# Last attention tiles and the next stages of a vision-transformer block: roots in three batches, a scale worked out early, a matrix inversion moved among products

## The reference

```python
h = patches @ w + b, with the class rows and the positions             # 32 x 38 x 256
h = h + attention(layernorm(h))                                        # 16 heads of 16, causal, q and k normalised
xn = layernorm(h) * gamma + beta
abel_out = gelu(xn @ abel_w + abel_b)
logits = xn @ moe_gate_w + moe_gate_b
topw, topi = top_k(logits, 2); topw = softmax(topw)                    # 8 experts
moe_out = sum over the two experts e of topw * (gelu(xn @ ew1[e] + eb1[e]) @ ew2[e] + eb2[e])
for i in range(3):
    moe_out = moe_out @ expm(gens[i])                                  # 256 x 256 generators
gate = sigmoid(concat(abel_out, moe_out) @ gc_w + gc_b)
out = h + abel_out * (1 - gate) + moe_out * gate
```

## Time and profile before

| | us |
|---|---|
| median of 3 runs | 394.57 (394.08 to 399.01) |
| the profiled execution | 394.72 |
| its span, from first to last instruction | 392.7 |
| TensorE busy in the span | 345.1 (88%) |
| VectorE, ScalarE, GpSimd busy | 214.8, 178.5, 151.4 |

### The profile page before, as it was taken

The page is one execution under the profiler, slowest core; times in us unless marked ns, Lnnn a source line. Parts: engine busy times, 40 slices in busy tenths (PEclk is TensorE's granted clock), DMA queues, the critical chain, the costliest instruction groups (busy, mean ns, idle before and its releaser), DMA issues.

```text
span 392.7 us, 6931 instructions
## 1 busy us (share of the span) xinstructions
PE 345.1 (88%) x2080; PEld 293.1 (75%) x2080; DVE 214.8 (55%) x581; ACT 178.5 (45%) x423; POOL 151.4 (39%) x168
## 2 busy tenths in 40 slices
PE   2998999769899999679986999999999999794894
PEld 2786454469788888556865899989999999693793
DVE  0237368797999999868785458421221123100175
ACT  1000354588998897335224844334434434341231
POOL 1002804050754663711041447653547446642000
PEclk9999899968999999969989999999999999989599
DMA  8741411133111100274222645523443444531442
GB/s 268 269 140 44 188 58 55 54 97 114 46 48 47 46 33 2 93 335 156 84 69 80 181 121 154 163 93 88 149 149 106 149 151 156 151 103 47 144 144 86
DMA packets 20544, 45.76 MB, mean 117 GB/s; under 512 B 2150, under 2 KB 12836, under 8 KB 20260
## 3 DMA queue, kind: packets, MB, share of 16 engines
q1 hardware_dynamic: 17732, 37.78, 29.1%
q0 software_dynamic: 2496, 6.82, 5.2%
q10 hardware_dynamic: 288, 0.81, 0.7%
HBM read 38.18 MB, written 7.22 MB: 116 GB/s over the span
## 4 chain that ended last, share of the span: by engine, by line
PE 75%; DVE 10%; issue 7%; DMA 3%; ACT 2%; POOL 1%; DVEq 0%; ACTq 0%; POOLq 0%; SPq 0%
PE banks L1422 11%; PE banks L1362 11%; PE banks L1431 10%; PE banks L1205 5%; PE banks L1175 5%; PE banks L1282 5%; PE banks L1258 4%; PE banks L1491 3%; PE banks L1300 3%; PE banks L1333 3%; PE banks L1501 2%; PE banks L1245 2%; PE banks L1191 2%; PE banks L1210 2%; PE banks L1231 2%
## 5 line engine op out<-in xcount | busy, mean ns | idle before, releaser
L1422 PE MATMUL banks<-qn_sb,w_sb 128*128 128x128 f32 x416 | 51.6, 278 | 1.0 <-ACT qn_sb L624 1.0
L624 ACT ACTIVATE qn_sb<-banks,col_sb 128x128 f32<-128x128 f32 x52 | 21.1, 458 | 66.1 <-PE banks L1409 66.1
L1431 PE MATMUL banks<-w_sb,sq_sb 128*128 x208 | 50.0, 385 | 0.3 <-ACT sq_sb L635 0.3
L1422 PEld LDWEIGHTS banks<-qn_sb,w_sb 128*128 128x128 f32 x416 | 49.2, 194 | 1.3 <-ACT qn_sb L624 1.2
L452 POOL DMA_INDIRECT y_rows<-pT_sb,sidx_sb x26 | 26.0, 999 | 56.7 <-DVE pT_sb L1097 55.5
L1431 PEld LDWEIGHTS banks<-w_sb,sq_sb 128*128 128x128 f32 x208 | 39.7, 194 | 5.7 <-issue 0.5
L1097 DVE TENSOR_TENSOR pT_sb<-banks,p_sb 128x256 f32<-128x256 f32 x26 | 11.0, 425 | 51.0 <-PE banks L1431 48.3
L635 ACT ACTIVATE sq_sb<-banks,col_sb 128x128 f32<-128x128 f32 x104 | 32.6, 369 | 12.9 <-PE banks L1422 10.8
L1175 PE MATMUL banks<-wtok_sb,patch_sb 128*114 128x256 f32 x132 | 30.4, 393 | 7.1 <-DMA wtok_sb<-in_w_tok 7.0
L446 POOL DMA_INDIRECT qn_sb<-z_rows,gidx_sb x26 | 27.4, 1054 | 21.1 <-PE banks L1409 14.1
L1175 PEld LDWEIGHTS banks<-wtok_sb,patch_sb 128*114 128x114 f32 x132 | 24.3, 186 | 12.8 <-DMA patch_sb<-in_patches 6.9
(11 more groups left out here) (204 smaller groups left out, 668.8 us busy)
## 6 DMA issues: line engine op xcount, KB each, us to landing
w_sb<-in_w SPq DMA_DIRECT2D x26, 512.0 KB
w_sb<-in_w SPq DMA_DIRECT2D x1, 4096.0 KB, 12.6
patch_sb<-in_patches SPq DMA_DIRECT2D x11, 342.0 KB, 3.0
vrep_sb<-v_rows SPq DMA_DIRECT2D x33, 114.0 KB
qk_sb<-y_rows SPq DMA_DIRECT2D x10, 228.0 KB
v_rows<-v_sb SPq DMA_DIRECT2D x11, 114.0 KB
z_rows<-h_sb SPq DMA_DIRECT2D x11, 114.0 KB
out_rows<-h_sb SPq DMA_DIRECT2D x10, 114.0 KB
```

The lines of the kernel that those rows point to most:

```text
L624: last = nc.scalar.activation(xsT_sb[:, (2 * s + c) * 128:(2 * s + c + 1) * 128], bank[1][:, c * 128:(c + 1) * 128], ACT.Identity, scale=c ...
L1422: last = nc.tensor.matmul(bank[2 + 2 * s + c // 2][:, (c % 2) * 128:(c % 2 + 1) * 128], w1_sb[:, w0:w0 + 128], xsT_sb[:, (2 * s + k) * 128 ...
L1431: last = nc.tensor.matmul(bank[6 + s][:, 0:D], hidT_sb[:, s * HID + k * 128:s * HID + (k + 1) * 128], w2_sb[:, ds(e * 4 * D + k * D, D)], ...
```

## The change

The roots (`powers`) are taken in three batches, tiles 0 to 6, 7 to 9 and 10 (`CUT = (7, 10)`), and the first comes ahead of `gather_images(9)` on GpSimd. The generators' scale is worked out by VectorE just ahead of the attention loop, and ScalarE multiplies by it, one copy at the end of each of its steps 8 and 9. VectorE prepares the first batch of roots after tile 8, puts `norm_z(0)` and `norm_z(1)` ahead of `select(10)`, and has the rest of the z stage in another order. On TensorE and ScalarE `turn_att(10)`, `output(10)` and `keep_attT(10)` stand later in the z stage; `rank()` comes after product 0 and `invert()` after product 6.

```diff
+        CUT = (7, 10)
 # GpSimd
             for t in range(NT):
+                if t == NT - 1:
+                    powers(1, 0, CUT[0])
                 if t >= 1:
                     gather_images(t - 1)
...
-            powers(1, 0, 8)
             gather_images(NT - 1)
-            powers(2, 8, NT)
+            powers(2, CUT[0], CUT[1])
+            powers(3, CUT[1], NT)
 # ScalarE, end of attn_step
+                if isinstance(t, int) and t in (8, 9):
+                    scale_generators(t - 8)
+
+            def scale_generators(n):
+                act.wait_ge(d_gen, 32)
+                act.wait_ge(scale_set, 1)
+                m = (a_sb, aT_sb[:, :])[n]
+                nc.scalar.activation(m, m, ACT.Copy, scale=nrm_sb[:, 12:13]).then_inc(n_scaled, 1)
 # ScalarE, z stage
             for t in range(NT):
-                if t == 3:
+                if t == 4:
                     keep_attT(NT - 1)
                 keep_zT(t, t % 2)
 # VectorE, attn_step
+                if isinstance(t, int) and t == NT - 1:
+                    norm_z(0)
+                    norm_z(1)
                 select(t, s)
-                if isinstance(t, int) and t == 9:
-                    aggregate(mv2_sb, 0, 8, NT, h1_stats)
-                    variances(0, 8)
-                    scale_generators()
+                if isinstance(t, int) and t == 8:
+                    aggregate(mv2_sb, 0, CUT[0], NT, h1_stats)
+                    variances(0, CUT[0])
 # VectorE: the 11 small instructions, without the two of line 913
-            def scale_generators():
-                dve.wait_ge(d_gen, 32)
+            def size_generators():
                 dve.wait_ge(n_max, 1)
...
-                link(nc.vector.tensor_tensor(nrm_sb[:, 12:13], nrm_sb[:, 9:10], nrm_sb[:, 11:12], ALU.add))
-                for m in (a_sb, aT_sb[:, :]):
-                    nc.vector.tensor_scalar(m, m, nrm_sb[:, 12:13], None, ALU.mult).then_inc(n_scaled, 1)
+                nc.vector.tensor_tensor(nrm_sb[:, 12:13], nrm_sb[:, 9:10], nrm_sb[:, 11:12], ALU.add).then_inc(scale_set, 1)
...
             shift(0, 0)
+            size_generators()
             attn_tiles(dve, attn_step)
 # VectorE, z stage (norm_z now waits for a batch of roots at tiles 0, 7 and 10)
-            for t in range(3):
+            for t in range(2, 5):
                 norm_z(t)
             finish(NT - 2)
-            norm_z(3)
+            aggregate(mv2_sb, CUT[0], CUT[1], NT, h1_stats)
+            variances(*CUT)
             keep_pre(0)
-            norm_z(4)
+            norm_z(5)
             keep_pre(1)
+            norm_z(6)
             finish(NT - 1)
-            aggregate(mv2_sb, 8, NT, NT, h1_stats)
-            variances(8, NT)
+            aggregate(mv2_sb, CUT[1], NT, NT, h1_stats)
+            variances(CUT[1], NT)
             for t in range(2, NT):
-                if t + 3 < NT:
-                    norm_z(t + 3)
                 keep_pre(t)
-                if t >= 4:
-                    top(t - 4)
-            for t in range(NT - 4, NT):
-                top(t)
+                if t + 5 < NT:
+                    norm_z(t + 5)
+                top(t - 2)
+            top(NT - 2)
+            top(NT - 1)
 # TensorE, z stage
             for t in range(NT):
-                if t == 3:
-                    turn_att(NT - 1, 0, False)
                 turn_z(t, t % 2)
                 if t == 0:
                     output(NT - 2, False)
+                if t == 3:
+                    turn_att(NT - 1, 0, False)
                 if t >= 1:
                     pre(t - 1, (t - 1) % 2)
-                if t == 3:
+                if t == 4:
                     output(NT - 1, False)
 # TensorE, products
-                if k == 1:
+                if k == 0:
                     rank()
-                if k == 5:
+                if k == 6:
                     invert()
```

More of the change, by code:

```diff
@@ L207, in vit_kernel @@
         residual_set, placed, onep_set, diag_set, e_widened = sem("residual_set"), sem("placed"), sem("onep_set"), sem("diag_set"), sem("e_widened")
-        n_part, n_max, n_scaled, v_staged = sem("n_part"), sem("n_max"), sem("n_scaled"), sem("v_staged")
+        n_part, n_max, n_scaled, scale_set = sem("n_part"), sem("n_max"), sem("n_scaled"), sem("scale_set")
         x_made, x_kept, x_turned, x_evac, p_made, y_set = (
@@ L910, in scale_generators, with norm_z @@
                 link(nc.vector.tensor_tensor(nrm_sb[:, 11:12], nrm_sb[:, 10:11], nrm_sb[:, 10:11], ALU.subtract))
-                link(nc.vector.tensor_tensor(nrm_sb[:, 12:13], nrm_sb[:, 9:10], nrm_sb[:, 11:12], ALU.add))
-                for m in (a_sb, aT_sb[:, :]):
-                    nc.vector.tensor_scalar(m, m, nrm_sb[:, 12:13], None, ALU.mult).then_inc(n_scaled, 1)
+                nc.vector.tensor_tensor(nrm_sb[:, 12:13], nrm_sb[:, 9:10], nrm_sb[:, 11:12], ALU.add).then_inc(scale_set, 1)
+            def norm_z(t):
+                if t in (0,) + CUT:
+                    dve.wait_ge(rstd2, 1 if t == 0 else 2 + CUT.index(t))
+                nc.vector.tensor_scalar(h_sb[0:T, t * D:(t + 1) * D], h1_sb[0:T, t * D:(t + 1) * D], mv2_sb[0:T, 2 * t:2 * t + 1],
+                                        R[1][:, t:t + 1], ALU.subtract, ALU.mult).then_inc(zrow_set, 1)
             newton(1, 0)
@@ L925, in _ @@
             idx3 = idx_sb[0:T, :].rearrange("p (t k) -> p t k", k=8)
-            def norm_z(t):
-                if t in (0, 8):
-                    dve.wait_ge(rstd2, 1 + t // 8)
-                nc.vector.tensor_scalar(h_sb[0:T, t * D:(t + 1) * D], h1_sb[0:T, t * D:(t + 1) * D], mv2_sb[0:T, 2 * t:2 * t + 1],
-                                        R[1][:, t:t + 1], ALU.subtract, ALU.mult).then_inc(zrow_set, 1)
             def keep_pre(t):
```

## The result

| | before | after |
|---|---|---|
| median of the runs made together | 394.82 us (4 runs) | 384.79 us (4 runs) |
| profiled execution | 394.72 us | 385.5 us |
| its span | 392.7 us | 383.6 us |
| mean granted clock, share of full | 0.951 | 0.963 |

The ratio of the times is 0.973, with an interval from 0.966 to 0.980: faster by 2.7%. The eight runs of it lie between 384.4 and 389.1 us. The forecast of 386.6 us lies among them, and 384.79 lies in its range. The ratios leave out executions over 1.5% longer than the fastest of their kernel; the profiles of `before_new_products` and `best` show such executions, with half clock from 79 to 103 us, and only the stages behind that are read from them.

What follows compares the result with a forecast made beforehand. Bound: TensorE, 88% busy, so only its waits and half clock can be won: the 5.42 us gap before the z stage and those among the products. 5.4 + 2.6 - 0.05, about 8.0 us, gives 386.6 us; range 384.0 to 389.8.

Steps and rivals of the forecast that it cites:

- 0.3 us on the chain up to `pre(2)`: z stage: charge for three norm_z on VectorE colliding with GpSimd's sums; the full row would be 0.7 us.
- `pre(4)`'s new wait: z stage: TensorE waits 1.7 us, from 172.5, for keep_pre(2), placed behind finish(10) and the third batch's statistics.
- the seven last `pre`: End of the z stage: with five turns 7.3 us, plus 0.2 for the tie with VectorE, ending at 181.8.
- 2.1 of half clock gone: Start of the z stage: half clock from 169.4 to 173.6 goes with the gap, worth about 2.1 us.
- The 1.7 of half clock "that no longer follows": Products: 1.7 us of the 2.6 gained, from half clock that followed the waits within invert().
- the margin of 0.6: Start of the expert slots: their first rows' fetch lands at 208.3, slots start at 208.9, covered by 0.6 us.
- a fetch that releases `turn_xs(0)`: Start of the expert slots: sign of a wrong forecast, the trace naming the fetch as releasing the first transpose.
- rival C: Later stages: half-clock stretches fall otherwise, one gone is worth 1.6 us; 385.0 us; chance 0.15.
- A: z stage or products: half clock returns after the new wait at pre(4) or rank(), costing 1.6 us; 388.2; chance 0.20.
- the half microsecond between two of three runs: Earlier kernel's runs: two 0.5 us apart, taken as evidence against time scattering with the clock window's phase.
- B: Products: only the first part pays; rank()'s wait, then clock or fetch take the rest; 389.2 us; chance 0.10.
- D: z stage: runs at 1.2 GHz throughout, 12.1 us more; 398.7 us, or 414.3 with products too; chance 0.03.

Runs made afterwards that it cites:

- before_new_products: Kernel before the change with rank() after product 0 and invert() after product 6, nothing else; 391.34 us, ratio 0.994.
- best: Changed kernel with both z-stage reorderings, invert() after product 5, TensorE's register read moved earlier, and unread matmuls in waits behind the products; 380.89 us, ratio 0.966.
- scale_only: Kernel before with only the scale worked out ahead of the loop and applied by ScalarE; 391.23 us, ratio 0.993.
- z_keep0: Changed kernel with keep_pre(0) put ahead of finish(9) and the second batch's statistics; 388.1 us, ratio 0.985.
- z_keep23: Changed kernel with keep_pre(2) and keep_pre(3) put ahead of finish(10); 386.6 us, ratio 0.983.
- scale_back: Changed kernel with the scale again worked out and applied on VectorE after tile 9; 390.85 us, ratio 0.994.
- after_old_products: Changed kernel with rank() after product 1 and invert() after product 5, as before; 388.41 us, ratio 0.983.

## Why the prediction was right, and where it was not

**The start of the z stage: right.** 164.98 for 164.8, `norm_z(0)` at 162.95 for 163.0, ScalarE's copies 1.57 and 1.56 for 1.5, `values(10)` at 162.98 for 163.0. The roots took 2.64 us for 14 columns, not 3.1: the slope came from a row of 3.45 for 16 columns that ran beside VectorE's two multiplications; `scale_only` shows 2.95 for the same 16. It changed nothing, as ScalarE's second copy came last. Ahead of the loop VectorE's line 840 starts at 91.09 instead of 91.05: 0.04 for 0.05.

**Inside the z stage: the step that failed.** I said 17.0 us from `turn_z(0)` to the end of the last `pre` and got 18.05 (183.03). The forecast had 0.3 us on the chain up to `pre(2)`, for the three `norm_z` beside `gather_images(10)`; `pre(2)` waited 0.85. Two things make that wait. The collision came in full, 1.94 us as in the earlier trace rows, 0.7 more than three at 0.4. And the forecast had no term for the second batch's statistics, 0.62 us, which the new order puts ahead of `keep_pre(0)`; it had counted the third batch's ahead of `keep_pre(2)`. `z_keep0` shows that the order is enough: with the collision unchanged, `pre(2)` doesn't wait once `finish(9)` and the statistics stand behind. The other half of the miss is small terms: `pre(4)`'s new wait was 1.81 for 1.7, and the seven last `pre` took 7.8 us for 7.5. `z_keep0` and `z_keep23`, which shift the two waits, shorten the stage by 0.4 and 1.2.

I had quoted the Trainium skill (GPSIMD Engine Reference, Specifications), by which GpSimd and VectorE share their memory interfaces and contend for them. The trace agrees for the sums of `gather_images`: 1.94 us for three `norm_z` beside them, and 0.83 for a sum instead of 0.73. It shows no cost beside the roots: while they run from 169.76 for 1.34 us, two `norm_z` take 0.40 each, as they do alone. The full 0.7 was nearer than my 0.3.

Seen as a whole, the forecast charged the new order of the stage with 1.3 us: 2.1 of half clock gone, and only 0.8 gained (17.8 to 17.0). The half clock did go, and the stage got 0.2 longer, so by these rows the order costs an estimated 2.3 us at full clock. `scale_only` beside `scale_back` shows 1.0 of it, where both begin at half clock and `pre(2)` waits only 0.19.

**The products: right as a sum, by parts not all.** From the end of the last `pre` to the first `turn_xs` 21.50 us (183.03 to 204.53) for 21.7; 1.20 at `rank()` for 1.25; none at `invert()`. The 1.7 of half clock "that no longer follows" did go, but not by the order: `after_old_products` and `scale_only` have the old waits in `invert()` and full clock. It moves between executions, and what the lists give without it is 1.1 us, of which the two places are 0.7.

**The fetch and the tail.** It landed 5.31 us after its issue, 0.5 over the forecast, which used up most of the margin of 0.6. So the sign "a fetch that releases `turn_xs(0)`" came, by less than 0.2 us; the interval of 1.12 us behind the last evacuation, the same with a fetch 8.7, 7.1 and 5.5 us ahead, shows that TensorE's own list ended there as well.

**Slots and output.** Said to be the same, shown 2.1 shorter, and 1.2 longer in the second profile. That is rival C, and A seen from the other side: half clock from 205 to 216 in one execution and not in another of one kernel. By the Trainium skill (TensorE: Matmul & The Clock Gate, Part 1) the window runs freely, and both would be matters of phase. Eight runs of one kernel between 384.4 and 389.1 us agree with it, though no run here tells phase from another cause that changes between executions. I had given too much weight to the half microsecond between two of three runs. Rivals B and D are out: the second part paid, and the clock was 1.00 in the z stage throughout.

Put together, what the change itself is worth is 4.5 us at the start, -0.2 in a z stage that is no longer at half clock, and 1.1 (2.8 with the half clock gone) in the products. That is 5.4 to 7.1 for the 8.0 forecast. The mechanism at the start and in the products was right and the z stage was too good by 1.0; that the measured time lies so near is in part luck, since the slots' 2.1 us made up for it in the first four runs and did not in the second four (387.15).

One sum of the rivals is off: the range of 384.0 to 389.8 is said to take in B with A, which would be 390.8 (389.2 + 1.6).

## What to carry to other kernels

When an engine's queue is shortened, list everything that then stands in the new order between a buffer's producer and its release, with collisions at the full price of the row. And price the new order by itself: here the earlier start gained 4.5 us, and the new order of the next stage cost 1.0 where two runs show it alone, which the total hides. Cut both executions at common events before explaining a total, and run the same kernel twice, since a stage with the same list can differ by more than the effect looked for. A releaser that a trace names may only be the last of several things that end together; move it and see whether the end moves.

## What the hardware showed unexpectedly

- The half-clock stretches move between executions of one kernel: none between 205 and 216 us in one, then 205 to 216 at 0.53 in the other, where the expert slots and the output took 3.4 us more of some 385.
- Where the wait ahead of the output stage was filled with matmuls, TensorE's work in the stage ran at full clock instead of at half for its first 6 us (0.88 in the mean). The stage took 25.83 us instead of 27.10 with 14 of them, and 24.45 with 28, but then it began 4.4 us late.
- A TensorE matmul of 128x256 in f32 took 0.44 us (28 in 12.25) and stood as two records.
- A register read on TensorE after its last wait cost 0.76 us on the path; no row of the trace shows it as work.
- GpSimd's `pow` is slow for its size, and nearly linear in it: 0.70 us for 2 columns, 1.34 us for 6 columns, 2.64 for 14, 2.95 for 16, and 3.45 for 16 beside VectorE's copies.
